# Scale factors from exponent bits, and the order of TensorE's last products, in three bisection sweeps

## What is computed

```python
h = relu(layernorm(x))
L_norm = d_inv_sqrt[:, None] * L * d_inv_sqrt[None, :]
_, U = eigh(L_norm)                       # eigenvectors, ascending eigenvalues
x = x + U @ (relu(U.T @ h @ W1 + b1) @ W2 + b2)
h = relu(layernorm(x))
h = relu(adj @ (h @ Wg0 + bg0)); h = relu(adj @ (h @ Wg1 + bg1))
for p in 1..4:                            # windows of p rows through an LSTM, last state back into h
    h[:, p-1::p] = lstm_last(Wih[p-1], Whh[p-1], ..., windows(h, p))
x = x + h
```

## Time and profile before

| | |
|---|---|
| median of 3 runs | 1576.59 us (1576.54 to 1576.85) |
| profiled execution | 1576.68 us, of which the span from first to last instruction 1574.9 us |
| mean granted TensorE clock | 0.944 |
| busy: PE, DVE, ACT, POOL | 1226.0, 1252.9, 650.1, 359.5 us |

### The profile page before, as it was taken

How to read it: one execution, slowest core, us unless ns; L and a number is a source line. 1 busy time by engine, 2 the same in 40 slices (tenths; PEclk the granted TensorE clock), 3 DMA queues, 4 the chain that set the end, 5 groups by cost and what they waited for, 6 DMA issues and landing times.

```text
span 1574.9 us, 25121 instructions
## 1 busy us (share of the span) xinstructions
PE 1226.0 (78%) x5747; PEld 1006.4 (64%) x5747; DVE 1252.9 (80%) x6155; ACT 650.1 (41%) x2370; POOL 359.5 (23%) x1884
## 2 busy tenths in 40 slices
PE   6888889999976667777354454374999999999998
PEld 4666677777765555555243333262778789999997
DVE  7999999988888888888999999997682255555555
ACT  2333333443443444322121222250234587968676
POOL 5233323333345555555200000002000001010100
PEclk9999999999999999999967776787999999999999
DMA  7000000000000000000000000000000000001012
GB/s 174 2 1 1 1 1 1 1 1 2 1 1 1 1 1 1 1 1 1 1 0 1 1 0 1 0 1 0 1 1 1 0 1 1 1 1 28 1 28 55
DMA packets 23403, 12.63 MB, mean 8 GB/s; under 512 B 5075, under 2 KB 22230, under 8 KB 23254
## 3 DMA queue, kind: packets, MB, share of 16 engines
q1 hardware_dynamic: 23254, 11.03, 2.9%
HBM read 6.83 MB, written 4.19 MB: 7 GB/s over the span
## 4 chain that ended last, share of the span: by engine, by line
DVE 56%; PE 32%; issue 9%; ACT 2%; DVEq 1%; POOL 0%; POOLq 0%
PE bank L842 8%; DVE A L1081 5%; PE bank L844 5%; PE bank L851 4%; DVE RC L1169 4%; DVE O L1177 3%; DVE junk L1014 3%; DVE zc L1075 3%; DVE wk L1065 3%; DVE pa L1165 3%; DVE pc L1038 3%; DVE O L1173 3%; PE pair L842 2%; DVE gqn L1052 2%; DVE A L1071 2%
## 5 line engine op out<-in xcount | busy, mean ns | idle before, releaser
L490 ACT ACTIVATE ncp<-pc,RC 128x2 f32<-128x2 f32 (+1 forms) x254 | 74.9, 295 | 305.7 <-DVE RC L1041 305.7
L699 PE MATMUL bank<-O,y 128*128 128x2 f32 x510 | 142.3, 349 | 65.3 <-DVE y L1014 59.9
L629 ACT ACTIVATE H<-bank,gate_b 128x128 f32<-128x128 f32 (+2 forms) x468 | 167.4, 467 | 50.8 <-PE bank L844 37.8
L684 PE MATMUL bank<-ident,O 128*128 128x128 f32 x382 | 148.2, 457 | 51.4 <-DVE O L1058 38.1
L699 PEld LDWEIGHTS bank<-O,y 128*128 128x128 f32 x510 | 127.8, 311 | 77.7 <-issue 71.9
L684 PEld LDWEIGHTS bank<-ident,O 128*128 128x128 f32 x382 | 60.1, 197 | 139.4 <-DVE O L1058 139.4
L707 PE MATMUL pair<-ident,pc 128*128 128x128 f32 x381 | 145.2, 450 | 4.4 <-DVE pc L1038 1.1
L842 PE MATMUL bank<-O,WlT 128*128 128x128 f32 (+1 forms) x672 | 144.9, 326 | 4.6 <-DVE O L1445 2.8
L774 PE MATMUL bank<-chg,fold 128*128 128x512 bf16 x64 | 29.9, 594 | 139.2 <-DVE chg L1127 139.2
L319 POOL TENSOR_TENSOR ym<-y,below 128x2 f32<-128x2 f32 (+1 forms) x254 | 49.6, 195 | 349.9 <-DVE y L1024 249.9
L1071 DVE SCALAR_TENSOR_TENSOR A<-pair,cx,A 128x254 f32<-128x254 f32 (+63 forms) x380 | 121.3, 319 | 0.4 <-issue 0.2
(11 more groups left out here) (444 smaller groups left out, 3444.6 us busy)
## 6 DMA issues: line engine op xcount, KB each, us to landing
X<-in_x SPq DMA_DIRECT2D x2, 2048.0 KB, 13.1
out<-X SPq DMA_DIRECT2D x32, 128.0 KB, 1.9
adj_sb<-in_adj SPq DMA_DIRECT2D x1, 256.0 KB, 3.0
W1s<-in_L_gnn_W SPq DMA_DIRECT2D x1, 64.0 KB, 11.1
W2s<-in_L_gnn_W SPq DMA_DIRECT2D x1, 64.0 KB, 4.1
Wg0s<-in_L_gnn_Wg SPq DMA_DIRECT2D x1, 64.0 KB, 3.9
Wg1s<-in_L_gnn_Wg SPq DMA_DIRECT2D x1, 64.0 KB, 3.7
Wl<-in_L_gnn_Wih SPq DMA_DIRECT2D x1, 0.5 KB, 6.9
```

The lines of the kernel that those rows point to most:

```text
L490: a(ncp[:, bs], pc[:, bs], ACT.Identity, scale=RC[:, k, 1:2]).then_inc(S["ncp_ready"], 1)
L629: ins = a(gates[:, q, i, 0:n], gate_at(p, q, i), fn, bias=gate_b[:, p - 1, i:i + 1])
L684: ins = nc.tensor.transpose(xb[:, b * P:(b + 1) * P], R[:, b, k, 0:1].to_broadcast([P, P]), idf)
L699: ins = mm(sb_[:, 0:2], y[:, 1:2].to_broadcast([P, P]), R[:, 1, k, :], start=True, stop=(k >= P - 1))
```

## The change

L1196 becomes a bitwise AND of the 32-bit pattern with 0x7F800000, which leaves a power of two (or zero) from the exponent. L1200, the reciprocal, becomes integer arithmetic on the same pattern: times -1, plus 0x7F000000, which is the pattern of the inverse power of two. Both are one `tensor_scalar` (`ts`) on tiles read as int32. On PE the two products with `corr` and the wait for `corr_ready` go behind the last products with `chg`.

```diff
+I32 = mybir.dt.int32
@@ tensor engine, end of a sweep
-                        pe.wait_ge(S["corr_ready"], s + 1)
-                        for o in range(2):
-                            mm(bank[0][:, 0:w], fold[:].rearrange("p a r -> p (a r)"), corr[:, 0:w], start=False, stop=False)
                     pe.wait_ge(S["chg_ready"], n + 1)
                     g = 512 // w
                     for q in range(2):
                         for o in range(8 * (n % 2), 8 * (n % 2) + 8, g):
-                            last = mm(bank[0][:], fold[:].rearrange("p a r -> p (a r)"), chg[:, q, o:o + g, 0:w], start=(n == n0 and q == 0 and o == 0),
-                                      stop=(n + 1 == n1 and q == 1 and o == 16 - g))
+                            last = mm(bank[0][:], fold[:].rearrange("p a r -> p (a r)"), chg[:, q, o:o + g, 0:w], start=(n == n0 and q == 0 and o == 0), stop=False)
+                    if n + 1 == n1:
+                        pe.wait_ge(S["corr_ready"], s + 1)
+                        for o in range(2):
+                            last = mm(bank[0][:, 0:w], fold[:].rearrange("p a r -> p (a r)"), corr[:, 0:w], start=False, stop=(o == 1))
                     last.then_inc(S["sweep_ps"], 1)
@@ vector engine, steps 32/60 and 33/61
-                        mark(ts(pm[:, :, 0:w], pm[:, :, 0:w], TINY, None, ALU.max))
+                        mark(ts(pm[:, :, 0:w].bitcast(I32), pm[:, :, 0:w].bitcast(I32), 0x7F800000, None, ALU.bitwise_and))
-                        mark(v.reciprocal(pr[:, :, 0:w], pm[:, :, 0:w]))
+                        mark(ts(pr[:, :, 0:w].bitcast(I32), pm[:, :, 0:w].bitcast(I32), -1, 0x7F000000, ALU.mult, ALU.add))
```

## The result

| | before | changed |
|---|---|---|
| median of 5 runs | 1576.85 us (1576.54 to 1577.31) | 1570.53 us (1569.93 to 1571.11) |
| profiled execution, span | 1576.68, 1574.9 us | 1570.60, 1568.7 us |

The ratio is 0.9961, with a 95% interval of 0.9949 to 0.9972: 6.3 us faster. 1571.0 was forecast, with 1569.7 to 1572.6 as range. The forecast took off 5.6 us, from a median of 1576.59; the medians here are 6.3 apart. The interval reaches from about 4.4 to 8 us, so the times alone don't tell terms of a few tenths apart; the traces do, because inside one execution the distance of two starts holds to some hundredths.

A forecast was written before the change was run, and what follows sets the result against it. DVE was taken to bound the sweeps, except at the first sweep's end, where PE's products do. Gains of 0.32, 2.74 + 0.91 and 1.26 + 0.34 sum to 5.57 us: 1576.59 to 1571.0 us, range 1569.7 to 1572.6.

The forecast's parts named there:

- Price of the reciprocals: L1200, twice a sweep on DVE: replacing each reciprocal gives 0.63 us on narrow values and 1.37 us on wide ones.
- Integer forms: Both integer instructions on DVE in the sweeps were taken to cost 0 extra, as one-source operations like L1196.
- rival at one value per cycle: Integer forms on DVE run at about one value per cycle: 0.9 us less gain, 1571.9 us; chance 0.15.
- slow path: Integer operations on DVE run at the reciprocal's rate: 4.6 us lost, 1580.0 us in all; chance 0.03.
- First sweep: End of sweep 1: PE's wy(7) products cover the second reciprocal; gain 0.32 us, ends -0.9 and 1.47.
- cover gone: Sweep 1: clock rises early or is high when wy(7) begins; 1.15 us more gain, 1569.9 us; chance 0.12.
- Second sweep: Two wide reciprocals give 2.74 us; moving the corr products behind chg on PE gives 0.91 at sum L1231.
- 0.3 us to spare: End of sweep 2: the moved corr products on PE finish about 0.3 us before DVE's sum L1231 needs them.
- Third sweep: Two narrow reciprocals give 1.26 us, and the move on PE at sum L1231 gives 0.34 us.
- Behind the sweeps: Everything shifts as it stands; a later clock rise at the ten products L820 costs up to 0.5 us, taken as 0.
- late clock: Clock rises later, in the wy(7) block or at L820: 0.5 to 1.7 us less, 1571.5 to 1572.7; chance 0.08.
- idle move: The corr products, now last on PE, end as late as L774 did: 1.25 us less, 1572.3 us; chance 0.03.

The follow-up runs named there:

- the second profile: The changed kernel, unaltered, measured and profiled once more: 1570.88 us against 1577.28 for the kernel before, ratio 0.9960.

## Why the prediction was right

**Price of the reciprocals.** Right. From one L1196 (now L1197) of a sweep to the next, in which one reciprocal falls, the changed kernel is 0.64, 1.39 and 0.65 us shorter in sweep 1, 2 and 3 (0.63, 1.37, 0.63 forecast). The distance of starts was the right measure: by the durations it would have been 0.72 and 1.46. Both reciprocals of sweep 2 give 2.71 with the old order at the high clock (106.19 to 103.48) and 2.75 with the new one (106.21 to 103.46); 2.74 was forecast.

**Integer forms.** Taken at no extra cost; 220 and 283 ns, so right. The rival at one value per cycle (0.15) and the slow path (0.03) are out. The Trainium skill's table (VectorE: DVE Perf Modes, The perf-mode tier table) names fp32 and bf16 only; the trace shows that int32 goes at the same rate, for the AND as well as for multiply and add.

**First sweep.** 0.32 forecast, 0.48 in the profile of the changed kernel, with the chain through L648 and the wait at L1222 as described. The distance was to grow to about 1.3 us and grew to 1.16. The prediction's own reckoning gives the difference: measured from L1135, PE's block began 0.66 us earlier, and the rise of the clock, which the prediction held at its place, came 0.33 earlier (840.66 - 770.71 against 839.86 - 770.24, from half a microsecond around each rise); the end of the block moves by half of their sum, 0.50. The term is not one number, though, and that this profile came near 0.32 is luck. In the second profile there was no wait and the sweep was 0.92 shorter, 1.40 below before: the rival "cover gone" (0.12) happened in an execution of the same program. PE's block on the timeline of the second profile and DVE behind it:

```profile
837.02 2.98 PE L648 MATMUL bank<-Pm,PmT 128*128 128x256 f32 x8
839.84 1.89 PE L648 MATMUL bank<-PmT,Pm 128*128 128x256 f32 x8
...
843.05 0.22 DVE L1222 TENSOR_TENSOR O<-O,bank 128x64 f32<-128x64 f32 x1
```

2.98 and 1.89 us, where the first profile has 3.62 and 2.25. The clock rose 3.0 us behind PE's first products after its pause there (836.20 to 839.2) and 5.0 us behind them in the first profile (834.91 to 839.9). Over the four profiles with old reciprocals sweep 1 is 73.75 to 74.37 us long, over the six with the integer forms and `wy(7)` in its old place 72.56 to 73.96: against the mean of the old ones (73.96) 0.5 gained on the average, between 0 and 1.4. All of it lies inside the ends that the prediction gave, -0.9 to 1.47. The Trainium skill (TensorE: Matmul & The Clock Gate, What's actually happening) has the gate look on a schedule of its own; the runs agree, since the same program meets its rise at different places.

**Second sweep.** The sum was right, 3.65 forecast and 3.65 measured, but the step behind 0.91 of it failed. The prediction put the wait down to PE's order, with the products at the low clock, and took it as the move's alone. The experiments show that the old order alone makes no wait, only with the low clock does it: it is gone with the order of before and a filler (106.19), gone with the integer forms and the order of before (103.48), and back at 0.81 when PE is kept idle. That the number came out is luck in so far as either part of the change would have taken the wait away.

Why the integer forms come with the high clock isn't shown. All eight profiles with integer forms and a whole `wy(15)` have it at the second end; of the two with old reciprocals and no filler, one has. DVE arrives 1.4 us earlier with the integer forms, and PE's pause ahead of the exchange is 0.7 to 1.5 us in these eight, against 2.92 in the kernel before. But with the move alone the pause is almost as long, and the clock stayed high (from 947.5 to 961.2 us, where in the kernel before it was high from 946.5 to 953.3 only):

```profile
951.87 0.70 PE L766 MATMUL pair<-O,sel 128*128 128x256 f32 x2 [2.92 <-DVE O L1208]
```
```profile
952.48 0.70 PE L767 MATMUL pair<-O,sel 128*128 128x256 f32 x2 [2.72 <-DVE O L1209]
```

So the length of this pause alone doesn't tell the clock behind it, and where the clock falls against PE's work is a matter of the single execution here as well. In executions with the high clock the move gives nothing in sweep 2 (103.46 to 103.49 with it, 103.48 and 103.49 without). The "0.3 us to spare" of the `corr` products was also reckoned for one state only; with a low clock through the exchange as well they are 0.37 late.

**Third sweep.** Right: 1.26 + 0.34 forecast, 1.62 measured, and here the two parts do add (1.27 and 0.33 alone). PE has no `wy` near this end, and the clock was low there in all profiles.

**Behind the sweeps.** The ten products with no reader met a later rise (4.8 us behind their start instead of about 3.3), as was possible, and took 6.98 us instead of 5.94, with the next six right behind:

```profile
1077.28 6.98 PE L821 MATMUL bank<-WlT,ident 128*128 128x512 f32 x10 [25.48 <-DVE junk L1345]
```

It cost nothing that could be seen: from the end of the last `lo` to the end of the span there are 541.5 us (541.4 in the second profile), and 541.4 before. So the total was right by terms that were right, but for the 0.91, which was put down to one part of the change where two could take it, and the 0.32, which one profile met and another did not.

The prediction's sentence that the gain falls below 3.15 only when the slow integer rate, a late clock and an idle move come together is too strict by its own terms: 5.57 less 0.9 and 1.7 is 2.97, and less 1.7 and 1.25 it is 2.62, so two of them are enough. Of the three only a later rise came, at L820, and it cost nothing that could be seen.

What stays open: what the move gives where the exchange is still at the high clock and the four products behind it are at the low one, as in the profile of before. By the durations it would be the 0.9 of the prediction, an estimate; no profile with the new order showed that state.

## What to carry to other kernels

Before a wait for PE is put down to the order of its work, look at its clock there: compare the duration of the products behind the wait with the same ones elsewhere (here 1.91 and 1.03 us), and read the granted clock of the stretch. The gains of two changes that each remove the same wait must not be added; whoever forecasts them writes down which wait each one takes. Where a block on another engine and the main engine arrive within a microsecond of each other, one profile shows one of two outcomes. Moving the block to where that engine has time took the wait and most of the scatter (five runs within 0.19 us instead of 1.18 and 1.26), and brought about as much in the median, 0.3 us, as the reordering brought in the third sweep.

## What the runs showed of the hardware

- Bitwise AND, AND with XOR, and multiply with add on int32 views take about as long on DVE as a float maximum: 215 to 222 ns for 128x128 and 280 to 290 ns for 128x256 by the means of nine profiles (the maximum 216 to 222 and 288); a reciprocal takes 943 and 1744.
- A filler of twelve instructions (2.75 us) on an idle PE came with a high clock for four later products, 1.03 us instead of 1.91, and with a sweep shorter by 0.92, as much as the reordering gave.
- The place of the clock's rise against the same work moved by about 2 us between two executions of one program, and with it the end of a stage by 0.9 us, while the two later sweeps agreed within 0.03 us.
- Two pauses of PE of almost the same length (2.92 and 2.72 us) were followed by a low clock in one program and a high one in another.
